# LSTM cell update folded into scale and bias of ScalarE's sigmoid, in a graph layer on one Trainium2 core

## The reference

```python
x_proj = einsum('btd,gd->btg', x, W_ih) + b_ih + b_hh
def step(carry, xp):                       # 6250 times, one after the other
    h, c = carry
    gates = xp + h @ W_hh.T                # 1024 values
    i, f, g, o = split(gates, 4)
    c = sigmoid(f) * c + sigmoid(i) * tanh(g)
    h = sigmoid(o) * tanh(c)
    return (h, c), h
logits = hs @ W_lin.T + b_lin              # which of two: g = argmax
w = g * hs;  inc = cumsum(w);  prefix = inc - w;  suffix = inc[-1] - inc
out = 2 * hs + prefix * fw_att + suffix * bw_att
```

## Time and profile before

| | us |
|---|---|
| median of 3 runs | 18018.25 (18016.04 to 18020.35) |
| the profiled execution's own time | 18005.85 |
| its span, first to last instruction | 18003.9 |
| busy in the span: PE / DVE / ACT / POOL | 14961.4 / 7375.8 / 6807.2 / 2722.7 |

### The profile page before, as it was taken

One profiled execution on the slowest core, in us unless ns is written; L12 is line 12 of the kernel. 1 busy time (PEld: TensorE's weight loads), 2 busy tenths in 40 slices (PEclk: granted clock), 3 DMA queues, 4 the chain that ended last, 5 costly groups with the idle time before them and its releaser, 6 DMA issues. The chain is left out here.

```text
span 18003.9 us, 1832831 instructions
## 1 busy us (share of the span) xinstructions
PE 14961.4 (83%) x837380; PEld 13287.0 (74%) x837380; DVE 7375.8 (41%) x47174; ACT 6807.2 (38%) x36128; POOL 2722.7 (15%) x4549
## 2 busy tenths in 40 slices
PE   2367576767311999999999999999999999999994
PEld 1356465655201899999999999999999999999993
DVE  2465656556334333333333333333333333333335
ACT  1244353535211244444444444444444444444441
POOL 0165463726310000000000000000000000000000
PEclk9978788888655999999999999999999999999996
DMA  0143352424311100000000000000000000000000
GB/s 22 40 126 116 90 154 62 145 70 135 117 56 37 49 2 2 2 2 2 2 2 2 2 2 2 2 2 2 2 2 2 2 2 2 2 2 2 2 2 15
DMA packets 720915, 580.96 MB, mean 32 GB/s; under 512 B 579762, under 2 KB 631100, under 8 KB 708536
## 3 DMA queue, kind: packets, MB, share of 16 engines
q1 hardware_dynamic: 482385, 316.90, 6.1%
q0 software_dynamic: 238400, 262.61, 5.6%
HBM read 325.17 MB, written 252.12 MB: 32 GB/s over the span
## 5 line engine op out<-in xcount | busy, mean ns | idle before, releaser
L1342 PE MATMUL p_g<-ring,wh 128*32 128x32 f32 x800000 | 8266.6, 197 | 2.3 <-issue 2.3
L1342 PEld LDWEIGHTS p_g<-ring,wh 128*32 128x32 f32 x800000 | 7571.2, 108 | 801.2 <-DVE ring L1437 414.8
L1431 DVE CUSTOM_DVE_ANT_1 cj<-cell 128x4 f32<-128x4 f32 x12500 | 2037.8, 163 | 6796.8 <-ACT cell L1384 6796.8
L1384 ACT ACTIVATE cell<-p_g 128x3 f32<-128x3 f32 x12500 | 2172.9, 174 | 6691.9 <-PE p_g L1342 6691.9
L1320 PE MATMUL p_g<-xq,idn 128*128 128x6 f32 (+2 forms) x15006 | 2495.7, 262 | 13.4 <-PEq L1330 13.4
L1387 ACT ACTIVATE tc<-cell 128x1 f32<-128x1 f32 x12500 | 2482.3, 199 | 0.0
L1437 DVE SCALAR_TENSOR_TENSOR ring<-og,tc 128x1 f32<-128x1 f32 x12500 | 1924.0, 159 | 755.9 <-ACT og L1395 1.5
L1466 POOL COPY hist<-ring 128x6 f32 x2501 | 475.6, 190 | 11569.2 <-POOLq L1465 11569.2
L1320 PEld LDWEIGHTS p_g<-xq,idn 128*128 128x128 f32 x15006 | 2049.0, 189 | 218.6 <-issue 13.6
L297 POOL DMA_INDIRECT eb<-node_tab,eidx x1650 | 2059.0, 1248 | 627.4 <-issue 446.1
L1325 PE MATMUL p_f<-wh,idn 128*128 128x128 f32 (+1 forms) x7500 | 2043.6, 354 | 0.0
(11 more groups left out here) (205 smaller groups left out, 8154.4 us busy)
## 6 DMA issues: line engine op xcount, KB each, us to landing
edge_tab<-eb SPq DMA_DIRECT2D x96, 1391.1 KB
edge_tab<-eb SPq DMA_DIRECT2D x96, 758.8 KB
eb<-node_tab,eidx POOLq DMA_INDIRECT x1650
xp_tab<-xo SPq DMA_DIRECT2D x50, 500.0 KB, 2.6
xq<-xp_tab SPq DMA_DIRECT2D x1251, 8.0 KB, 1.7
xq<-xp_tab SPq DMA_DIRECT2D x1250, 12.0 KB, 1.7
x<-w_in SPq DMA_DIRECT2D x8, 1024.0 KB
node_tab<-hrow SPq DMA_DIRECT2D x50, 126.0 KB
```

The costliest lines, as they stand in the source:

```text
L1342: m = pe.matmul(to[32 * q:32 * q + 32], wh[:, k, D * q + 32 * c:D * q + 32 * c + 32], ring[:, (s - 1) % TS, k:k + 1].broadcast_to([128, W] ...
L1384: act.activation(cell[:, s, k, 0:6:2], gate_at(h, u, k)[:, :, 0], ACT.Tanh).then_inc(l_s[k], 1)
L1431: dve.tensor_tensor_reduce(cj[:, k, :].rearrange("p (a b) -> p a b", a=2), cell[:, s, k, 0:4].rearrange("p (a b) -> p a b", a=2), cell[:, ...
```

## The change

The cell is no longer finished before its tanh. DVE makes two factors a half, `cf` (in the trace `cfac`): `cf[0] = (tanh(i/2) + 1) * tanh(g)` and `cf[1] = (tanh(f/2) + 1) * 0.5`. ACT then computes `sigmoid(cf[1] * cell + cf[0])`, with the old cell as input, `cf[1]` as scale and `cf[0]` as bias, both read from SBUF, one value a partition. The cell in memory is twice the true one, so that this sigmoid less one half is tanh(c)/2. DVE computes the cell itself (`new_c`) behind `new_h(1)`, for the next step. Gate o becomes a true sigmoid, `ring` holds h/2 in place of 2h, and the factors in the weights and in the last stage go with that.

```diff
@@ ScalarE, each step
                             def gates(k):
-                                act.activation(cell[:, s, k, 0:6:2], gate_at(h, u, k)[:, :, 0], ACT.Tanh).then_inc(l_s[k], 1)
+                                act.activation(gt[:, s, k, 0:6:2], gate_at(h, u, k)[:, :, 0], ACT.Tanh).then_inc(l_s[k], 1)
                             def tanh_c(k):
-                                return act.activation(tc[:, (s % 2), k:k + 1], cell[:, (s + 1) % TS, k, 5:6], ACT.Tanh)
+                                return act.activation(tc[:, (s % 2), k:k + 1], cell[:, s, k:k + 1], ACT.Sigmoid, bias=cf[:, s, k, 0:1], scale=cf[:, s, k, 1:2])
...
-                            act.activation(og[:, (s % 2), :], gate_at(h, u, 2)[:, :, 0], ACT.Tanh).then_inc(l_o, 1)
+                            act.activation(og[:, (s % 2), :], gate_at(h, u, 2)[:, :, 0], ACT.Sigmoid).then_inc(l_o, 1)
@@ VectorE, each step
+                            def factors(k):
+                                g_ = gt[:, s, k, :].rearrange("p (a b) -> p a b", b=2)[:, :, 0]
+                                dve.scalar_tensor_tensor(cf[:, s, k, :], g_[:, 0:2], 1.0, g_[:, 2:4], ALU.add, ALU.mult).then_inc(l_c[k], 1)
+
                             def new_c(k):
-                                dve.tensor_tensor_reduce(cj[:, k, :].rearrange("p (a b) -> p a b", a=2),
-                                                         cell[:, s, k, 0:4].rearrange("p (a b) -> p a b", a=2),
-                                                         cell[:, s, k, 4:6].unsqueeze(2).broadcast_to([128, 2, 2]),
-                                                         0.5, 0.0, ALU.mult, ALU.add, cell[:, (s + 1) % TS, k, 5:6]).then_inc(l_c[k], 1)
+                                return dve.scalar_tensor_tensor(cell[:, (s + 1) % TS, k:k + 1], cell[:, s, k:k + 1], cf[:, s, k, 1:2], cf[:, s, k, 0:1],
+                                                                ALU.mult, ALU.add)
                             def new_h(k):
-                                dve.scalar_tensor_tensor(ring[:, s, k:k + 1], og[:, (s % 2), k:k + 1], 1.0, tc[:, (s % 2), k:k + 1],
-                                                         ALU.add, ALU.mult).then_inc(l_h[k], 1)
+                                dve.scalar_tensor_tensor(ring[:, s, k:k + 1], tc[:, (s % 2), k:k + 1], 0.5, og[:, (s % 2), k:k + 1],
+                                                         ALU.subtract, ALU.mult).then_inc(l_h[k], 1)
                             dve.wait_ge(l_s[0], s + 1)
-                            new_c(0)
+                            factors(0)
                             dve.wait_ge(l_s[1], s + 1)
-                            new_c(1)
+                            factors(1)
...
                             new_h(1)
+                            for k in range(KC):
+                                new_c(k)
@@ once, before the loop
-                            a = dve.tensor_scalar(w_[:, c], w_[:, c], 0.5 if c in (2, 5) else 0.25, None, ALU.mult)
+                            a = dve.tensor_scalar(w_[:, c], w_[:, c], 2.0 if c in (2, 5, 6, 7) else 1.0, None, ALU.mult)
@@ last stage, 50 times
-                        dve.tensor_tensor(h, h, wv_[:, k, 0:TS_], ALU.add).then_inc(s_dve, 1)
+                        dve.scalar_tensor_tensor(h, h, 4.0, wv_[:, k, 0:TS_], ALU.mult, ALU.add).then_inc(s_dve, 1)
```

More of the change, by code:

```diff
@@ L1207, in _ @@
                     dve.sem_inc(s_dve, -1)
-                    dve.memset(gsc[:, 2:6:3], 1.0).then_inc(s_dve, 1)
+                    dve.memset(gsc[:, 2:6:3], 1.0)
+                    dve.memset(gsc[:, 6:8], 1.0).then_inc(s_dve, 1)
                     dve.wait_ge(s_dve, 1)
@@ L1217, in _ @@
                         for n in range(GT):
-                            a = dve.tensor_scalar(wi[:, k, n, :].rearrange("p (q r) -> p q r", q=4), v_[:, n], 1.0 if n in (2, 5) else 0.5,
+                            a = dve.tensor_scalar(wi[:, k, n, :].rearrange("p (q r) -> p q r", q=4), v_[:, n], 1.0 if n in (2, 5, 6, 7) else 0.5,
                                                   None, ALU.mult)
@@ L1261, in gps_kernel @@
                 ring = sb(sub, "ring", [128, TS, KC])
-                cell = sb(sub, "cell", [128, TS, KC, 6])
+                cell = sb(sub, "cell", [128, TS, KC])
+                gt = sb(sub, "gtan", [128, TS, KC, 8])
+                cf = sb(sub, "cfac", [128, TS, KC, 2])
                 og, tc = sb(sub, "og", [128, 2, KC]), sb(sub, "tc", [128, 2, KC])
-                cj = sb(sub, "cj", [128, KC, 4])
                 part_of = ((0, 3), (3, 6), (6, 8))
@@ L1377, in _ @@
                     act.wait_ge(l_z, 1)
-                    act.activation(tc[:, 0, :], tc[:, 1, :], ACT.Tanh)
+                    act.activation(tc[:, 0, :], tc[:, 1, :], ACT.Sigmoid)
                     with act.Fori(0, IT):
@@ L1407, in _ @@
                     dve.sem_inc(s_dve, -1)
-                    dve.memset(cell[:, :, :, 1:4:2], 1.0).then_inc(s_dve, 1)
+                    dve.memset(gt[:, :, :, 6], 0.5).then_inc(s_dve, 1)
                     dve.wait_ge(s_dve, 1)
@@ L1541, in _ @@
                 dve.sem_inc(s_dve, -1)
-                dve.tensor_scalar(wl[:], wl[:], 0.5, None, ALU.mult).then_inc(s_dve, 1)
+                dve.tensor_scalar(wl[:], wl[:], 2.0, None, ALU.mult).then_inc(s_dve, 1)
                 dve.wait_ge(s_dve, 1)
@@ L1560, in _ @@
                         h = hist[:, k, cols]
-                        dve.scalar_tensor_tensor(wv_[:, k, 0:TS_], h, 0.5, gl[:, 0:TS_], ALU.mult, ALU.mult).then_inc(s_dve, 1)
+                        dve.scalar_tensor_tensor(wv_[:, k, 0:TS_], h, 2.0, gl[:, 0:TS_], ALU.mult, ALU.mult).then_inc(s_dve, 1)
                         dve.wait_ge(s_dve, 1)
```

## The result

| | before | with the change |
|---|---|---|
| median of 4 runs, us | 18017.15 | 18165.79 (18156.52 to 18171.99) |
| ratio | 1 | 1.0082, 95% interval 1.0066 to 1.0098 |
| profiled execution, its span, us | 18003.9 | 18170.0 |

The account below looks back on a forecast made before the run. The chain of PE's products, `og` and `new_h(0)` bounds a step; two u = 0 steps, each 0.065 longer, add 0.13 us an iteration, x 1250 = 163 us on 18,018.25, giving 18,181 us; range 18,010 to 18,310.

Parts of the forecast that it names:

- What bounds a step: Each loop step: the last of PE's 64 products, `og` and `new_h(0)` form the chain; u = 0 steps take 1.81.
- The price of the operands: Cell activation on ACT: scale and bias read from SBUF add 178 ns to 199, making 377 ns, say 0.38 us.
- The low bound: Cell activation on ACT: two operands add 2 x 0.07 = 0.14, so it lasts 0.34; time 18,043 to 18,068 us.
- `og` at P + 1.44: Gate o on ACT, counted from PE's step start P: starts at 1.44 instead of 1.39, moving `new_h(0)` and restart by 0.05.
- Half 1 late: `new_h(1)` reaches PE at P + 2.14, putting its restart at 1.875: u = 0 steps 0.065 longer, filled steps unchanged.
- steps with a fill above 1.90: Sign in the u = 1 and u = 2 steps that the prediction is wrong upward.
- The middle between the two readings: When PE wants half 1: 0.25 to 0.28 after its restart, so a restart without stall at 1.86 to 1.89, taken as 1.875.
- The fills as cover: PE's `fill` in u = 1 and u = 2 steps: `new_h(0)` may be 0.09 and 0.07 later for nothing.
- DVE's cell updates: Two `new_c` behind `new_h(1)`, about 0.22 each, end by 2.52 before `factors(0)` at 2.81: hidden with 0.3 to spare.
- The sum: Whole loop: 2 x 0.065 = 0.13 an iteration, x 1250 = 163 us, giving 18,181 us, 0.9% slower.
- The rival that the operands are almost free: Cell activation up to 0.29, no cost for any duration below about 0.32; time 18,018 us; chance 0.17.
- Half 1 late in every step: From 0.39 the second cell activation is later than all fills; at 0.42 710 us more, 18,728 us; chance 0.15.

Follow-up runs that it names:

- the second group: Kernel before, both operands read from SBUF for one half's tanh only: half 1 18,182.08 us (ratio 1.0091), half 0 18,118.83 us (1.0056).
- the fourth group: Fills cut to 64 (u = 1) and 192 columns (u = 2): kernel before 17,768.63 us (ratio 0.9876), changed kernel 18,057.64 us (1.0035).

## Why the prediction was right, point by point

The chain, the price of the operands and the time came out as forecast. One step didn't, the place at which the late half 1 costs.

- **What bounds a step** (products, gate o, `new_h(0)`): right. Lengthening only what stands before gate o on ACT made PE's restart as late as gate o's end (0.04; 97 us for half 0 alone), and steps of 1.81 everywhere without fills show that nothing longer than this chain binds in the kernel before. With the change the path of half 1 decides as well, as the second group shows.
- **The price of the operands**, 0.38 from the row with both of them and 250 columns: measured 382 ns. The low bound, twice the 0.07 of the one-column row, was too low; one operand costs about 90 ns here. The Trainium skill's figure of about 93 ns for each such operand ("ScalarE: Activation LUTs", What ACT_TABLE_LOAD costs) comes within a few ns of both measurements: an estimate by it is 0.385 for two operands, where 0.382 was measured, and 0.292 for one, where 0.286 was.
- **`og` at P + 1.44**: right to 0.01. Being 13 ns shorter (160 against 173) in the queue it made `new_h(0)` 0.04 late instead of 0.05, and the restart 1.85.
- **Half 1 late**: the size was right by luck, the place was wrong. The prediction let the late half 1 push back the restart behind a u = 0 step, to 1.875, and kept the steps with a fill unchanged; it named steps with a fill above 1.90 as a sign of being wrong upward. They came: the u = 1 steps, which follow the u = 0 steps, take 1.911. PE restarts at 1.848, as `new_h(0)` lets it, and then stalls at the 33rd weight load. That stall lies ahead of the fill, among the products of the u = 1 step, so the fill doesn't cover it. The pair is 1.848 + 1.911 where the prediction had 1.875 + 1.89, 3.76 in both. The middle between the two readings, 0.265 after the restart, was a choice and not a row. The load is wanted at 0.248; it came at 0.283, 0.035 late, and cost 0.017. So about 0.018 of lateness cost nothing, which the prediction couldn't know, and 0.248 + 0.018 happens to be its 0.265.
- **The fills as cover**: right for the late `new_h(0)`, in u = 1 and u = 2, and the fourth group shows it; not for the stall of half 1, as said. The same change costs 149 us with them and 289 with small ones.
- **DVE's cell updates**: 0.22 each expected, 213 ns measured, hidden; with and without them 18,166.
- **Last stage**: the new instruction takes 420 ns, like the one it replaces, so zero.
- **The sum**: 0.13 an iteration against 0.12 measured; 163 us against 149. For each u = 0 step and the one behind it the forecast had 0.05 of late restart and 0.015 for half 1; measured were 0.043 and 0.017. The first is smaller because of the shorter `og`.
- **The rival that the operands are almost free** fell to the measured 382 ns. Its condition, no cost below about 0.32, was borne out at one point, 0.286. **Half 1 late in every step** didn't come about with the fills; it did in the run with the small ones, where every step takes 1.86 to 1.87.

## What to carry to other kernels

Two operands read per partition made a short activation twice as long, and in a latency chain it matters where the added time falls: read it not from the instruction itself but from what stands behind it on its queue and from the slack of the second chain. Such a cost can have a threshold: here one operand was free and two weren't. And two late paths that met at the same engine cost the larger of the two here, not the sum. Before trading instructions on the engines with idle time, look at what the busy one does behind its last useful product: cutting the filler work gained more here (315 us) than this change cost.

## What the runs showed of the hardware

- A scale of 1 and a bias of 0 that are read from SBUF cost the same 183 ns as real factors (382 against 199 ns in both runs), and either operand alone about 90 (286 against 199 ns, 128 x 1). The next activation started 0.28 behind the one with both, against 0.07 behind a gate activation of 0.17.
- An activation of 2 columns from PSUM takes 160 ns when it stands in the queue behind a long one and 172 to 173 when a semaphore from PE releases it, for tanh and sigmoid alike.
- A weight load on PE that came 0.035 late cost its step 0.017 (with the change), and one that came 0.086 late cost 0.068 (operands for half 1 alone): in both some 0.018 of lateness cost nothing. Why wasn't tested.
- PE at 91% busy by the profile, with pauses in every step, kept its granted clock of 1.00 through the loop.
